# Attention scores with two heads in two 64-row halves of TensorE, maxima of two heads read at once, and the value products moved into the middle of the next step

## What is computed

```python
x = x + 0.5 * ffn(layernorm(x))      # 4-bit weights, 256 -> 2048 -> 256, gelu(gate) * up
q, k, v = (h @ Wq.T + bq), (h @ Wk.T + bk), (h @ Wv.T + bv)      # 16 heads of 16
scores = einsum('bqhd,bkhd->bhqk', q, k) * 16 ** -0.5
attn = softmax(where(causal, scores, min))
x = x + einsum('bhqk,bkhd->bqhd', attn, v).reshape(B, S, H) @ Wo.T + bo
x = x + 0.5 * ffn(layernorm(x))
```

## Time and profile before

| what | us |
|---|---|
| median of three runs | 1139.37 |
| the profiled execution | 1138.86 |
| its span, first to last instruction | 1137.2 |
| TensorE matmul busy | 1082.1 (95%) |
| VectorE busy | 694.4 (61%) |
| ScalarE busy | 582.9 (51%) |

### The profile page before, as it was taken

How to read it: one execution, slowest core, us unless ns; L and a number is a source line. 1 busy time by engine, 2 the same in 40 slices (tenths; PEclk the granted TensorE clock), 3 DMA queues, 4 the chain that set the end, 5 groups by cost and what they waited for, 6 DMA issues and landing times. The chain is left out here.

```text
span 1137.2 us, 17563 instructions
## 1 busy us (share of the span) xinstructions
PE 1082.1 (95%) x6448; PEld 710.4 (62%) x6448; DVE 694.4 (61%) x1606; ACT 582.9 (51%) x1112; POOL 112.1 (10%) x409
## 2 busy tenths in 40 slices
PE   4999999998998999999999999999989999999998
PEld 3888888886875433333333333333358888888887
DVE  5986545447465577887888888888333434344333
ACT  5764443432334645656677776777752433324222
POOL 1000000000001226231111111111100000000000
PEclk9999999998998889999999999999999999999999
DMA  6001030250030911322022202200000000000000
GB/s 191 2 21 28 10 120 1 48 149 1 13 119 1 229 34 39 81 52 52 1 53 53 50 3 53 52 2 1 1 1 1 1 4 16 1 19 1 19 1 19
DMA packets 75223, 43.81 MB, mean 39 GB/s; under 512 B 47161, under 2 KB 68993, under 8 KB 75137
## 3 DMA queue, kind: packets, MB, share of 16 engines
q1 hardware_dynamic: 75137, 42.68, 15.2%
HBM read 25.63 MB, written 16.78 MB: 37 GB/s over the span
## 5 line engine op out<-in xcount | busy, mean ns | idle before, releaser
L1010 ACT ACTIVATE attn_prob<-psum 128x512 f32<-128x512 f32 (+3 forms) x640 | 301.5, 540 | 145.4 <-PE psum L694 141.6
L1153 DVE TENSOR_REDUCE attn_part_max<-psum 128x1 f32<-128x512 f32 x384 | 244.0, 685 | 56.8 <-PE psum L709 54.9
L606 PE MATMUL psum<-ffn_xt,all_w_hi 128*128 128x512 f32 x512 | 166.1, 406 | 0.0
L753 PE MATMUL psum<-attn_prob,attn_vals 128*32 128x512 f32 (+3 forms) x1280 | 160.5, 556 | 4.1 <-ACT attn_prob L1010 2.9
L1349 PE MATMUL psum<-ffn_xt,all_w_hi 128*128 128x512 f32 x512 | 160.5, 395 | 2.4 <-DVE ffn_xt L1486 2.4
L1156 DVE CUSTOM_DVE_ANT_0 attn_junk<-psum,attn_mask 128x128 bf16<-128x128 f32 (+3 forms) x256 | 117.3, 486 | 27.9 <-PE psum L709 27.3
L1496 DVE TENSOR_TENSOR ffn_act_out<-ffn_act_out,psum 128x512 f32<-128x512 f32 x64 | 44.1, 689 | 108.4 <-ACT ffn_act_out L1419 108.4
L621 PE MATMUL psum<-all_w_hi,ffn_inner 128*128 128x256 f32 x512 | 105.0, 288 | 0.1
L1349 PEld LDWEIGHTS psum<-ffn_xt,all_w_hi 128*128 128x128 f32 x512 | 92.9, 190 | 18.9 <-DVE ffn_xt L1486 2.6
L606 PEld LDWEIGHTS psum<-ffn_xt,all_w_hi 128*128 128x128 f32 x512 | 92.7, 192 | 16.5 <-issue 0.3
L1419 ACT ACTIVATE ffn_act_out<-psum 128x512 f32<-128x512 f32 x64 | 38.4, 599 | 125.7 <-PE psum L1349 124.9
(11 more groups left out here) (138 smaller groups left out, 1529.9 us busy)
## 6 DMA issues: line engine op xcount, KB each, us to landing
qk_rows<-qkv_parts SPq DMA_DIRECT2D x16, 384.0 KB, 2.6
qk_rows<-qkv_parts SPq DMA_DIRECT2D x16, 256.0 KB, 3.0
attn_q_early<-qk_rows SPq DMA_DIRECT2D x8, 384.0 KB, 4.4
attn_q_late<-qk_rows SPq DMA_DIRECT2D x8, 384.0 KB, 3.9
attn_k_mid<-qk_rows SPq DMA_DIRECT2D x3, 768.0 KB, 7.1
attn_k_late<-qk_rows SPq DMA_DIRECT2D x3, 768.0 KB, 6.9
all_x<-in_L_attn_h SPq DMA_DIRECT2D x4, 512.0 KB, 6.2
v_rows<-qkv_rows_v SPq DMA_DIRECT2D x16, 128.0 KB, 2.6
```

The lines of the kernel that those rows point to most:

```text
L606: last = nc.tensor.matmul(psum[:, 2 * m + q % 2, :], w_part[a][:, 3 * g + m, pl, o:o + P], xt[:, b % 2, c, pl, :], start=(n == 0), stop=(n ...
L753: last = nc.tensor.matmul(psum[r:r + 32, O0, at:BT], vals[:, k0 * SUB + kb + k, 2 * hd:2 * hd + 32], prob[:, (4 * d + 2 * k + hd) % PRING, ...
L1010: nc.scalar.activation(prob[:, n % PRING, at:BT], psum[:, S0 + n % SBANKS, at:BT], ACT.Exp).then_inc(s["exp"], 1)
L1153: nc.vector.tensor_reduce(to, psum[:, bank, :], AX.X, ALU.max).then_inc(s["max_read"], 1)
```

## The change

- Queries and keys are kept as two fp32r parts, three products a head: 48 rows (`KR`) and two rows of maximum. Head 0 of a pair is in rows 0 to 49 and head 1 in rows 64 to 113 of the same tile, so a score has 50 rows and starts at row 0 or 64. The factor 1/4 moves into the Exp.
- A chunk's matmul of one head is now a `half`. Behind a score of head 0 stands the half of head 1, and the other way round. The two halves go to two neighbouring banks, and VectorE reads both with one reduce. On the diagonal the mask is added by two more matmuls (identity times a 128 x 128 mask), and the reduce is the ordinary one.
- PSUM: three banks for scores and for `turn_max`, in one ring (so `turn_max` takes a place in it); two pairs of banks for chunks and `gather`, in another.
- `gather` and `weigh(d - 1)` now stand behind score 1 of step d.
- A unit needs one op of ScalarE and one of VectorE, where it was three and two; a maximum is split in two parts. The constant rows are written once to DRAM.
- The 24 early chunks are spread anew: 3,2,3,2 and 2,3,3,3,3 in the turns 1 to 4 and 11 to 15 of the last block.

```diff
-NPART = 3
-Q_PARTS = (0, 0, 0, 1, 1, 2)
-K_PARTS = (0, 1, 2, 0, 1, 0)
-KR = len(Q_PARTS) * HD
+NPART = 2
+KR = 3 * HD
...
+            def halves_behind(d, j):
+                mine = [e for e, a in enumerate(chunk_at) if a == d]
+                if j < 2:
+                    return [(e, 1 - j) for e in mine[:1]]
+                if len(mine) == 2:
+                    return [(mine[1], 3 - j)]
+                return [(e, hd) for e in mine[j - 1::2] for hd in (3 - j, j - 2)]
...
+                def head(hd, n):
+                    return slice(HALF * hd, HALF * hd + n)
...
-                            part = slice(0, KR + NPART)
+                            part = head(hd, KR + NPART)
...
+                            bank, part = pair_bank("max", e), head(hd, KR)
...
+                            last = nc.tensor.matmul(psum[:, bank + hd, 0:cols], queries(b)[part, g % 2 * BT + i * P:g % 2 * BT + (i + 1) * P],
+                                                    keys(k0 + c)[part, 0:cols], start=True, stop=(c < qt), skip_group_check=True)
+                            if c < qt:
+                                last.then_inc(s["max_scored"], 1)
+                            elif place == 1:
+                                for a in range(2):
+                                    nc.tensor.matmul(psum[:, bank + a, cols - P:cols], identb[:, :], mask[:, :], start=False, stop=True,
+                                                     skip_group_check=True).then_inc(s["max_scored"], 1)
...
                         for d in range(NS):
                             for j in range(4):
                                 score(d, j)
-                                for e, hd in maxima_behind(d, j):
-                                    maxima(2 * e + hd)
+                                for e, hd in halves_behind(d, j):
+                                    half(e, hd, taken.get(e, 0))
...
-                                if j == 2 and gathered(d) is not None:
+                                if j == 1 and gathered(d) is not None:
                                     gather(gathered(d))
-                            if d >= 1:
-                                weigh(d - 1)
+                                if j == 1 and d >= 1:
+                                    weigh(d - 1)
...
-                            if c < qt:
-                                nc.vector.tensor_reduce(to, psum[:, bank, :], AX.X, ALU.max).then_inc(s["max_read"], 1)
...
+                            dve.wait_ge(s["max_scored"], 2 * e + 2)
+                            nc.vector.tensor_reduce(part_max[:, g % 2, :, i, c], psum[:, bank:bank + 2, 0:cols], AX.X, ALU.max
+                                                    ).then_inc(s["max_read"], 1)
```

More of the change, by code:

```diff
@@ L46 @@
 SBANKS = 3
-MBANKS = 3
 PRING = 8
@@ L186, in front @@
             EARLY = 4
-            N_EARLY = 2 * sum(1 for g, _, _ in chunks if g < EARLY)
+            N_EARLY = sum(1 for g, _, _ in chunks if g < EARLY)
             def quota(d):
@@ L425, in _ @@
                             load_x(b)
+                        sp.wait_ge(s["made"], 1)
+                        for kind in range(2):
+                            for at in (0, 4):
+                                constant_rows(kind, at)
                         sp.wait_ge(s["w_lo"], JOBS)
@@ L697, in maxima, with pair_free @@
-                        def maxima(n):
-                            e, hd = divmod(n, 2)
+                            nc.tensor.matmul(psum[:, single_bank("score", 4 * d + j), at:BT], keys(k0 + c)[part, o * P:(o + 1) * P],
+                                             queries(b)[part, g % 2 * BT + at:g % 2 * BT + BT], start=True, stop=True).then_inc(s["scored"], 1)
+                        def pair_free(kind, n):
+                            u = pair_use[kind, n]
+                            if u < 2:
+                                pe.wait_ge(s["lo"], NU * NB)
+                                pe.wait_ge(s["v"], SUB * NB)
+                                pe.wait_ge(s["added"], NB)
+                            elif pair[u - 2][0] == "max":
+                                pe.wait_ge(s["max_read"], pair[u - 2][1] + 1)
+                            else:
+                                pe.wait_ge(s["normed"], pair[u - 2][1] + 1)
@@ L733, in early_step @@
                             if kind == "max":
-                                maxima(n)
+                                half(n, 0, 0)
+                                half(n, 1, 1)
                             else:
@@ L1147, in maxima @@
                                 dve.wait_ge(s["row_max"], g - 1)
-                            if c == qt and any(b[2] == groups[b[0]][0] for b in chunks[:e]):
-                                before_it = max(f for f in range(e) if chunks[f][2] == groups[chunks[f][0]][0])
-                                dve.wait_ge(s["max_read"], 2 * before_it + hd + 1)
-                            dve.wait_ge(s["max_scored"], n + 1)
-                            if c < qt:
-                                nc.vector.tensor_reduce(to, psum[:, bank, :], AX.X, ALU.max).then_inc(s["max_read"], 1)
-                            else:
-                                cols = P * (i + 1)
-                                nc.vector.tensor_tensor_reduce(out=junk[:, hd, 0:cols], in0=psum[:, bank, 0:cols],
-                                                               in1=mask[:, BT - cols:BT], scale=1.0, scalar=START,
-                                                               op0=ALU.add, op1=ALU.max, accum_out=to).then_inc(s["max_read"], 1)
@@ L1242, in _ @@
                         norm(Q_USE[NB - 1])
+                        read = {}
                         for d in range(NS):
```

327 lines of the change are left out of this document (146 added, 181 removed).

## The result

The changed kernel takes 1297.42 us (median of four runs, 1289.54 to 1301.52) against 1138.9 for the kernel before on the same chip: a ratio of 1.1395, interval 1.1329 to 1.146. The forecast was 1154, its range 1115 to 1188. The direction held; the size was short by 143 us. The chip's executions of one kernel differ in how long the clock is at its lower level; where that matters, the clock of the execution stands beside its time. The profiled execution has a span of 1297.8 us (before 1137.2) and a mean granted clock of 0.870 (before 0.983).

A forecast was written before the change was run, and what follows sets the result against it. TensorE was taken to set the pace, and after the change a ring of waits. Second half +17, last pair +6, first half -6, -4 and -3, FFN -1, clock +6: +15 on 1138.86, 1154 us, range 1115 to 1188.

The forecast's parts named there:

- The ring: Plain full attention steps: a closed chain of waits through products, score 2 and two Exps, 2.72 us a step.
- score to Exp: Plain attention step: time from the start of score 2 to its Exp, 0.48 plus 0.10 for fp32r, 0.58 us.
- rival 2: Attention: the array's two halves don't run at once, some 46 us a pair, about 1197 us; chance 13%.
- The group's change: Second step of a group in the attention: products wait for gather, gather for copy; 4.27 us.
- The steps with a turn: Attention steps with `turn_max` in the scores' three banks: products 0.43 us later, two a pair, +0.9 us a pair.
- A pair at the upper level: Second half of the attention: 14 steps with turns and masks take 41.7 us, +2.4 a pair, seven pairs +17.
- The last pair: Last pair of heads, without chunks or turns: 39.6 us against about 33, +6 us.
- the early chunks (-1): 24 early chunks in the FFN: fewer waits for VectorE against tile switches and loads; -1 us, bounds -8 and +8.
- Clock: Attention, at changes of groups: thinner steps bring falls of 3.4 us costing about 1.2; +6 us, between 0 and 20.
- Rival 3: Attention: the clock falls at every change of groups, 32 falls at 1.2 to 2 us, about 1180 us; chance 10%.
- VectorE falls behind the ring everywhere: Attention: merged reads of 1.22 us give VectorE about 2.4 us a two-chunk step, under 2.72, so it doesn't bound.
- Steps 0 to 5, -3: First attention steps: eight fewer ScalarE ops of some 0.6 us for the last four units; -3 us, bounds 0 and 5.

The follow-up runs named there:

- the 64-row run: Kernel before with all scores and all maxima taken over 64 rows instead of 99 and 96: 1479.84 us, ratio 1.3041.
- Experiments 3 and 4: 3: kernel before, 64 rows in scores, 1257.18 us, or scores and maxima, 1479.84. 4: changed kernel, 128 rows in scores, 1817.92, or scores and halves, 1263.06.
- Short reads: Changed kernel with VectorE reading 128 columns of each bank of a chunk instead of up to 512: 1242.74 us; with all 128 rows too, 1206.3.

## Why the prediction was wrong, by its own steps

**Right.** The ring: 2.67 for 2.72; the term that is off is score to Exp, 0.53 where 0.58 was taken from the earlier trace rows. Score and half at once, against rival 2. Rival 2's price was sound: with no overlap (all 128 rows) a pair takes 44.90, for "some 46". The group's change goes through copy and gather, with the gather waiting for the copy; its second step takes 4.16 for 4.27, over 4 us as forecast. The steps with a turn take 3.31 and 3.10, 1.07 a pair over the plain ones, where 0.9 was written. A pair at the upper level costs 40.4 (forecast 41.7), +1.1 where +2.4 was written; had the clock held, the second half would have been better than forecast. The last pair was forecast 6 us longer; with the clock held by 128 rows it is (36.1 for 29.9). Of the early chunks (-1), nothing is seen against: ahead and behind the steps it is +0.5.

**The step that failed is "Clock", +6 with 20 as its upper bound.** It counted falls of 3.4 us, as the earlier trace rows has one, and took a clock of 1.00 in the thin last pair as a sign that thin steps alone don't lower it. Both readings left out that the steps before work with 96 to 99 rows and the new ones with 50, or 50 and 48. The changed kernel is at the lower level for 327 us of the attention (before 23). At 4.07 to 2.67 a microsecond there gives 0.34 back, so the 303 more come to about 104 us (an estimate). Two other readings agree with 0.34: the changed kernel's own executions (spans 1287.8 us at 0.879 and 1299.8 at 0.866, 12 us longer for 37 more at the lower level by these clocks, 0.33), and its last pair against the same with 128 rows (17.0 for 53.1, 0.32). Where TensorE was busy all the time, in the 64-row run, it is 0.46 (511.8 us for 274.9). Experiments 3 and 4 show the cause from both sides: fewer rows with a full queue go to the lower level and stay, and all rows in the changed kernel bring 327 us down to 72. In the full steps all rows also mean matmuls one behind the other, so rows and time at work change together there; the 64-row run in experiment 3 changes the rows alone. Rival 3 had the engine and the sign, with a price of 1.2 to 2 us a fall; the falls became stretches of up to 102 us. (Its sum was off as well: 32 falls at 1.2 to 2 in place of 6 give 1186 to 1212, not 1180, nearly all of it outside the range.) Rows alone don't decide either: the last pair of the two 64-row runs kept whichever level it came in with, and how the history counts isn't settled.

**"VectorE falls behind the ring everywhere" failed in the first half.** I counted its busy time for steps of two chunks, 2.4 under 2.72, and took -6 for the steps 12 to 47. Those take up to three chunks, in two pairs of banks that are free only after both heads are read. Short reads were worth 55 us in the changed kernel, of which some 40 are clock (116 us less at the lower level times 0.34) and 15 waits; with all 128 rows they were worth 57, of which 18 fall in steps that are at the upper level with and without them. The two causes feed each other: with shorter waits the same 50 rows are 116 us less at the lower level, and at that level the products take 1.87 for 1.00.

**"Steps 0 to 5, -3"** missed the buffer of the last unit: 8 us of stall, which the third buffer takes away. Step 0 also grew from 3.5 to 8.1 us, and did so in the kernel before with the move alone, where its products start 6.1 us earlier (354.8 for 360.9); in the changed kernel they start only 1.9 earlier.

**What is left over.** 160.6 us more in the profiled spans: about 104 clock, 8 the stall, 15 or more the waits for VectorE, 8 the seven pairs at +1.1, 6 the last pair's ring. That is 141. The other 20 aren't settled. The steps 6 to 47 have 197 us more at the lower level; if these gave 0.46 back instead of 0.34, it would be 24 more and cover them.

"TensorEngine Tiling (Array Packing)" of the Trainium skill (Key Properties), cited for the parallel tiles, says that tiles run in parallel: the trace agrees (score and half both start at 846.99). The drain that it names for a change of tiling mode shows too, as the 0.09 a change of the third experiment. The 2.0 us a step that came of the parallelism alone didn't: it is 2.67.

## What to carry to other kernels

Packing two small products into halves of TensorE's array frees time only if something can use it; where a ring of waits closes first, the engine works with fewer rows at the same pace, and its clock can fall for a hundred microseconds on end (102 here). Before halving the rows, look in the profile whether the clock row has falls already, and try the kernel as it is with narrower rows: that edit of a few lines (1480 us for 1139) shows the danger without the change, though not its size. Merging two reads into one saved little (1.22 us for two of 0.685), and it holds both banks until it ends, so count the ring of banks at the busiest step, not the mean.

## What was not expected of the hardware

- With 64 rows in scores and maxima and TensorE busy for 511.00 of 511.00 us in the second half, the granted clock was 0.50 (1.2 GHz) for 792 us on end; with 96 and 99 rows in the same instructions it was 1.00 in the second half.
- A change of tile between matmuls that share rows cost 0.09 us at the upper level (bf16) and 0.29 at the lower (fp32r, 0.72 for 0.43).
- The same last pair with 64-row scores went at 1.00 in one run and at 0.50 in another, each keeping the level that it came in with.
- Once at the lower level, the clock stayed there through full steps: 102.4 us on end in the changed kernel, with TensorE busy 93.49 of them.
